# Dequantizing weight tiles in full width of 512 columns, beside attention over 6272 keys

## What is computed

```python
x = x + xattn(layernorm(x), ctx_4096, ...)   # 32 query heads, 8 key/value heads of 128, 6272 keys
x = x + attn(layernorm(x), ...)              # four 512x512 and three 512x1792 quantized matrices, with LoRA
x = x + ffn(layernorm(x), ...)

def _dequant(codes, scales):                 # codes 0..15, one scale per 64 weights
    w = NF4[codes]
    O, I = w.shape
    w = w.reshape(O, I // BLOCK, BLOCK) * scales[:, :, None]
    return w.reshape(O, I)
```

## Time and profile before

| | us |
|---|---|
| median of three runs (range) | 1162.08 (1157.77 to 1168.44) |
| the profiled execution, whole time | 1156.21 |
| its span, first to last instruction | 1154.4 |
| PE busy | 1079.8 (94%) |
| DVE busy | 945.8 (82%) |
| POOL busy | 627.0 (54%) |
| ACT busy | 444.6 (39%) |
| stretch 0 to 52 us (prologue) | 52 |
| stretch 1055 to 1154 us (most of `tail`) | 99 |

### The profile page before, as it was taken

The page is one execution under the profiler, slowest core; times in us unless marked ns, Lnnn a source line. Parts: engine busy times, 40 slices in busy tenths (PEclk is TensorE's granted clock), DMA queues, the critical chain, the costliest instruction groups (busy, mean ns, idle before and its releaser), DMA issues. The chain is left out here.

```text
span 1154.4 us, 23709 instructions
## 1 busy us (share of the span) xinstructions
PE 1079.8 (94%) x7035; PEld 954.4 (83%) x7035; DVE 945.8 (82%) x2331; ACT 444.6 (39%) x993; POOL 627.0 (54%) x1303
## 2 busy tenths in 40 slices
PE   6889999999999999899999999999999999995587
PEld 4889989899899989799899889998999999982132
DVE  3358998889988889888899888999898998884365
ACT  2134444344443444334443434444434443431030
POOL 2036675665666666656656666657666556652100
PEclk9689999999999999999999999999999999996879
DMA  9512121112212122121221221212221111114991
GB/s 358 201 38 70 57 63 59 60 53 71 59 47 72 55 61 62 53 59 51 65 63 51 64 65 50 70 41 62 72 63 49 56 43 51 47 46 161 337 379 55
DMA packets 66852, 99.26 MB, mean 86 GB/s; under 512 B 7780, under 2 KB 34916, under 8 KB 65956
## 3 DMA queue, kind: packets, MB, share of 16 engines
q1 hardware_dynamic: 63954, 86.97, 23.9%
q10 hardware_dynamic: 2178, 8.34, 2.1%
q0 software_dynamic: 592, 2.40, 0.6%
HBM read 82.79 MB, written 14.89 MB: 85 GB/s over the span
## 5 line engine op out<-in xcount | busy, mean ns | idle before, releaser
L439 POOL TENSOR_SCALAR leaf<-bit 128x256 f32<-128x256 uint16 x896 | 402.4, 449 | 113.0 <-DVE bit L776 29.1
L788 DVE COPY_PREDICATED leaf<-bit,leaf 128x256 f32<-128x256 uint16 x784 | 388.4, 541 | 50.4 <-POOL leaf L439 14.6
L461 POOL TENSOR_TENSOR leaf<-leaf,scale 128x256 f32<-128x256 f32 x112 | 81.2, 735 | 185.3 <-DVE leaf L788 184.4
L644 ACT ACTIVATE v_hi<-p_kv 128x256 fp32r<-128x256 f32 x196 | 75.2, 384 | 175.6 <-PE p_kv L61 175.5
L59 PE MATMUL p_kv<-wkv_hi,ctx_even_hi 128*128 128x256 f32 x448 | 128.1, 286 | 5.6 <-DVE v_lo L727 4.6
L644 ACT ACTIVATE k_hi<-p_kv,bk_sb 128x448 fp32r<-128x448 f32 x112 | 70.8, 632 | 156.6 <-PE p_kv L61 156.1
L739 DVE TENSOR_TENSOR pt_lo<-p_t,pt_hi 128x512 fp32r<-128x512 f32 x224 | 128.8, 611 | 1.6 <-ACT pt_hi L655 1.2
L655 ACT ACTIVATE pt_hi<-p_t 128x512 fp32r<-128x512 f32 x224 | 115.0, 542 | 33.9 <-PE p_t L544 33.8
L60 PE MATMUL p_kv<-wkv_lo,ctx_even_hi 128*128 128x256 f32 x448 | 125.9, 281 | 0.0
L61 PE MATMUL p_kv<-wkv_hi,ctx_even_lo 128*128 128x256 f32 x448 | 125.7, 281 | 0.0
L727 DVE TENSOR_TENSOR v_lo<-p_kv,v_hi 128x256 fp32r<-128x256 f32 x196 | 82.2, 419 | 46.0 <-ACT v_hi L644 45.6
(11 more groups left out here) (190 smaller groups left out, 2523.7 us busy)
## 6 DMA issues: line engine op xcount, KB each, us to landing
code<-in_codes SPq DMA_DIRECT2D x56, 256.0 KB, 2.6
scale<-in_scales SPq DMA_DIRECT2D x112, 128.0 KB, 3.0
expanded_weights<-leaf SPq DMA_DIRECT2D x112, 128.0 KB, 1.7
wring<-expanded_weights SPq DMA_DIRECT2D x28, 512.0 KB, 12.5
ctx_st<-in_ctx_t SPq DMA_DIRECT2D x96, 112.0 KB, 2.1
wq_sb<-in_wq SPq DMA_DIRECT2D x8, 1024.0 KB, 14.0
wring<-in_wo SPq DMA_DIRECT2D x16, 512.0 KB, 12.4
stage<-in_wkv ACTq DMA_DIRECT2D x4, 1024.0 KB, 8.6
```

Source lines behind the costliest of these rows:

```text
L439: m = nc.gpsimd.tensor_scalar(leaf[:, b, slot, :], bit0[:, b * HW:(b + 1) * HW], NF4[2 * j + 1] - NF4[2 * j], NF4[2 * j], ALU.mult, ALU.add)
L461: nc.gpsimd.tensor_tensor(leaf[:, b, 4, :], leaf[:, b, 0, :], scale[:, b * HW:(b + 1) * HW], ALU.mult).then_inc(scaled, 1)
L644: nc.scalar.activation(dst, src, ACT.Identity, bias=0.0 if bias is None else bias).then_inc(kv_rounded, 1)
L788: return nc.vector.copy_predicated(leaf[:, b, slot, :], bit[:, b * HW:(b + 1) * HW], leaf[:, b, other, :])
```

## The change

`leaf` becomes five slots of the full 512 columns. Every select, leaf and scaling works on 128x512: 7 selects instead of 14, one scaling instead of two, one tile write instead of two. Of the eight leaves POOL keeps six, and ACT computes leaves 4 and 5 (`high_leaf`), with biases in a small tile that shares a buffer with `drop`. Semaphores are split up accordingly: `low_ready`, `high_act`, `high_pool`, `low_chosen`. The order on DVE, ACT, POOL and SP is new. The PE stream is unchanged.

```diff
-        leaf = sb(st, "leaf", [P, 2, 5, HW], F32)
+        leaf = sb(st, "leaf", [P, 5, TW], F32)
...
+            def high_leaf(n, k):
+
+                if k == 0:
+                    act.wait_ge(low_chosen, n + 1)
+                m = nc.scalar.activation(leaf[:, 1 + k, :], bit0[:], ACT.Identity, bias=high_base[:, k:k + 1],
+                                         scale=NF4[9 + 2 * k] - NF4[8 + 2 * k])
+                if k == 1:
+                    m.then_inc(high_act, 1)
...
                         if t == 1:
                             round_ctx(s, h, half, 0, last)
+                        if t in (3, 4):
+                            high_leaf(i, t - 3)
                 else:
+                    for k in range(2):
+                        high_leaf(i, k)
                     round_ctx(s, h, half, 3, last)
...
             def high_leaves(n):
+                wait_apart(pool, low_chosen, n + 1, pool_passed)
+                leaf_of(6, 3)
+                if not (isinstance(n, int) and n == 0):
+                    wait_apart(pool, weight_out, 16 * n, pool_passed)
+                leaf_of(7, 4).then_inc(high_pool, 1)
...
+            def high_by_bit1(n, part):
+                if part == 0:
+                    wait_apart(dve, high_act, n + 1, dve_passed)
+                    take(bit1, 1, 2)
+                else:
+                    wait_apart(dve, high_pool, n + 1, dve_passed)
+                    take(bit1, 3, 4).then_inc(choice, 1)
...
                 else:
-                    take_other_bits(i)
-                    low_by_bit1(i, 0)
-                    low_by_bit2(i, 0)
-                    low_by_bit1(i, 1)
+                    low_by_bit2(i)
...
+                if h % 2 == 1:
+                    for part in range(2):
+                        high_by_bit1(i, part)
+                    high_by_bit2(i)
+                    all_by_bit3(i)
                 split_keys(k_use(s, h, 0), k_bank(h, 0), nh, 0)
+                if h % 2 == 1:
+                    take_bit0(i + 1)
+                split_probs(i, 0)
+                split_probs(i, 1)
                 if h % 2 == 0:
-                    split_probs(i, 0)
-                    split_probs(i, 1)
-                    high_by_bit2(i, 1)
-                    all_by_bit3(i, 1)
-                else:
-                    low_by_bit2(i, 1)
-                    split_probs(i, 0)
-                    split_probs(i, 1)
-                    high_by_bit1(i, 0)
+                    low_by_bit1(i + 1, 0)
                 split_keys(k_use(s, h, 1), k_bank(h, 1), nh, 1)
                 if h % 2 == 0:
-                    take_bit0(i + 1)
+                    low_by_bit1(i + 1, 1)
                 split_probs(i, 2)
+                if h % 2 == 1:
+                    take_other_bits(i + 1)
                 split_probs(i, 3)
```

More of the change, by code:

```diff
@@ L375, in tile_out @@
             def tile_out(n):
-                for b in range(2):
-                    sp.wait_ge(scaled, 2 * n + b + 1)
-                    sp.dma_start(weights[n, :, b * HW:(b + 1) * HW], leaf[:, b, 4, :]).then_inc(weight_out[b], 16)
+                sp.wait_ge(scaled, n + 1)
+                sp.dma_start(weights[n], leaf[:, 4, :]).then_inc(weight_out, 16)
             codes_of(0, True)
@@ L393, in load @@
                             load_ctx(s + 1, piece + q, start and q == 0)
+                    more = not (last and pair == NKV // 2 - 1)
                     load(0)
-                    if not start:
-                        tile_out(n - 1)
-                        scales_of(n)
+                    if more:
+                        codes_of(n + 2)
                     load(1)
-                    if not (last and pair == NKV // 2 - 1):
-                        codes_of(n + 2)
-                    load(2)
                     tile_out(n)
                     scales_of(n + 1)
+                    load(2)
+                    if more:
+                        codes_of(n + 3)
                     load(3)
+                    tile_out(n + 1)
+                    if more:
+                        scales_of(n + 2)
                     load(4)
-                    if not (last and pair == NKV // 2 - 1):
-                        codes_of(n + 3)
                     piece += PAIR_PIECES[pair]
@@ L414, in _ @@
             chunk(NCH - 1, True)
-            tile_out(NB - 1)
-            for b in range(2):
-                sp.wait_ge(weight_out[b], 16 * NB)
+            sp.wait_ge(weight_out, 16 * NB)
         @block.gpsimd
@@ L445, in low_leaves @@
                 if not (isinstance(n, int) and n == 0):
[L446 to L448 removed]
+                    wait_apart(pool, scaled, n, pool_passed)
+                for j in range(3):
+                    leaf_of(j, j)
+                leaf_of(3, 3).then_inc(low_ready, 1)
             def high_leaves(n):
[L451 to L455 removed]
+                wait_apart(pool, low_chosen, n + 1, pool_passed)
[3 more added lines that the diff above has]
+                leaf_of(7, 4).then_inc(high_pool, 1)
             def apply_scales(n):
                 wait_apart(pool, scale_in, 32 * (n + 1), pool_passed)
[L459 to L462 removed]
+                wait_apart(pool, chosen, n + 1, pool_passed)
+                nc.gpsimd.tensor_tensor(leaf[:, 4, :], leaf[:, 0, :], scale[:], ALU.mult).then_inc(scaled, 1)
             def add_rowsum(i, h):
@@ L471, in add_rowsum @@
                 nc.gpsimd.tensor_tensor(denom[:, h, :], denom[:, h, :], rowsum[:, h % 4, :], ALU.add)
+            for j in range(2):
+                m = nc.gpsimd.memset(high_base[:, j:j + 1], NF4[8 + 2 * j])
+            m.then_inc(bases, 1)
             narrow(0, True)
@@ L482, in split @@
                             split_ctx(s + 1, piece + q, 1 - par)
-                    if not (isinstance(n, int) and n == 0):
-                        apply_scales(n - 1)
                     low_leaves(n)
+                    narrow(n + 1)
                     split(0)
                     high_leaves(n)
-                    narrow(n + 1)
                     add_rowsum(n, 2 * pair)
+                    apply_scales(n)
+                    low_leaves(n + 1)
                     split(1)
-                    apply_scales(n)
+                    if not (last and pair == NKV // 2 - 1):
+                        narrow(n + 2)
                     split(2)
-                    low_leaves(n + 1)
-                    split(3)
                     high_leaves(n + 1)
                     add_rowsum(n + 1, 2 * pair + 1)
-                    if not (last and pair == NKV // 2 - 1):
-                        narrow(n + 2)
+                    split(3)
+                    apply_scales(n + 1)
                     split(4)
@@ L675, in block_work @@
                 act.wait_ge(max_ready, i + 1)
-                nc.scalar.activation(alpha[:, par, :], drop[:], ACT.Exp).then_inc(alpha_ready, 1)
+                nc.scalar.activation(alpha[:, par, :], drop, ACT.Exp).then_inc(alpha_ready, 1)
                 for r in range(RT):
@@ L802, in high_by_bit1, with take @@
[L802 to L813 removed]
+            def take(bit, slot, other):
+                return nc.vector.copy_predicated(leaf[:, slot, :], bit[:], leaf[:, other, :])
@@ L887, in _ @@
                 block_work(NCH - 1, h, 0, False, True)
-            for b in range(2):
-                high_by_bit1(NB - 1, b)
-                high_by_bit2(NB - 1, b)
-                all_by_bit3(NB - 1, b)
             add_output(NB - 1, NKV - 1)
```

114 lines of the change are left out of this document (47 added, 67 removed).

## The result

The changed kernel takes 1330.18 us (median of 4 runs, 1327.31 to 1332.12) against 1163.35 for the kernel before on the same chip: ratio 1.143, interval 1.137 to 1.149. The profiled execution spans 1325.5 us, 171 more than before. The direction was predicted; 1215 and the range up to 1250 were not met.

The account below looks back on a forecast made before the run. PE was taken as the bound, DVE close behind. To the profiled 1156 us, odd blocks' loss of 73 less even blocks' return of 25 added 48, and half clock 11: 1215 us, range 1178 to 1250.

Parts of the forecast that it names:

- the place and the kind of the loss: Odd block: DVE waits 2.45 us for ACT's leaves, pt_lo comes late, PE is 2.7 us later per block.
- the prices of undisturbed work: 512-column instructions: select 0.73 us, ACT leaf 0.65, POOL leaf 0.65, scaling 1.27 to 1.47.
- bit 0 0.55 (0.590): Odd block, DVE between k_lo and the first pt_lo: bit 0's mask takes 0.55 us, from a row of 0.590.
- four masks to 545.2: Even block on DVE, after the last v_lo: three selects to 543.8, then four masks done at 545.2 us.
- four selects at 0.73 with POOL idle: Odd block, DVE: four selects on high leaves at 0.73 us each, since POOL has finished its leaves before ACT.
- the clock in one pair of three: Half clock behind PE's new stall in one pair of three: 9 x 1.3 = 11 us.
- the upper bound I gave: Bound on the half-clock loss behind PE's odd-block stalls: 27 x 1.4 = 38 us.
- even blocks 0.9 shorter: Even blocks: PE's 22.4 us of waits for v_lo, and a little more, come back, 0.9 us per pair.
- So 0 here: Even block after the last v_lo: the second k_lo starts at 548.4 us as before, so no change.
- with 0.5 gain ... and 1.0 loss: Bounds on the even block's tail: 0.5 us gain if POOL is quicker, 1.0 loss if its leaves take 0.90.
- +2.7 - 0.9 + 0.4 = 2.2: Per pair in us: odd block's loss 2.7, even block's return 0.9, the remaining term for half clock.
- Rival 2: Disturbed prices hold, selects 1.08 and POOL leaves 0.90 us, in odd blocks and even tails: 1280 us, chance 0.05.

Follow-up runs that it names:

- e7: Changed kernel with the odd tile's last low select moved into the even block before and ACT's two leaves ahead of the exponentials; 1208.41 us.
- e3: Kernel before with full-width leaves, selects, scaling and tile write alone, all leaves on POOL, old order as far as possible; 1169.93 us.
- e6: Changed kernel with POOL's scaling split into two instructions of 256 columns; 1314.77 us.
- e4: Changed kernel with POOL scaling only 2 of 512 columns and leaves made a thousand times smaller; 1249.54 us.
- e5: Changed kernel with bit 0 masked ahead of the last select, and the even blocks' other masks behind the second pt_lo; 1286.00 us.
- e1: Changed kernel plus 24 matmuls with unread results where PE waits in odd blocks; 1291.98 us.
- e10: Kernel of e5 with 16 of e1's filler matmuls in the odd blocks; 1276.33 us.
- e8: Changed kernel's full width and ACT leaves kept, order of all engines rewritten, only low selects ahead of pt_lo in odd blocks; 1137.35 us, 0.981 of the kernel before.
- e9: Kernel of e8 with leaves 4 and 5 on POOL again, nothing else changed; 1165.94 us.
- e2: Changed kernel with ACT's two leaves moved to POOL, ahead of its two high ones; 1318.40 us.

## Why the prediction was wrong where it was

**Right: the place and the kind of the loss.** The leaves of ACT were to end 4.0 us after `drop`; DVE's select behind them starts at 4.1. The idle time was to be 2.4 us, 28 times, 65 us in total; it is 2.7, 28 times, 76.7. Transposes of chunk 2 wait for `pt_lo`, odd blocks lose, even ones don't wait for `v_lo` any more. e7 confirms the mechanism by taking it away, and e3 shows that the order and not the width made the loss. The order on SP and POOL alone was not put to a test.

**Right: the prices of undisturbed work.** A select of 512 columns was put at 0.73 and takes 0.73 to 0.75, ACT's leaf at 0.65 and takes 0.7, POOL's leaf at 0.65 and takes 0.62, the scaling at 1.27 to 1.47 and takes 1.30.

**Wrong: bit 0 at 0.55 and each other mask at 0.28 ("bit 0 0.55 (0.590)", "four masks to 545.2").** Bit 0 takes 1.10 in the odd block, one mask of the even block some 1.4. I had used the mean of the kernel before without asking what made it nearly twice the other masks' 320. Both masks stand in the new order close behind the last select (in the odd block with one `k_lo` between), which is what POOL's scaling waits for. The Trainium skill, SBUF — State Buffer, section "SBUF: two separate sides", names beside DVE's instructions with two SBUF inputs those that run in a 2-port mode. By that rule a mask, which has one input, waits for the end of a POOL instruction that began before it, if it runs in such a mode. I had applied the rule only to selects. Rows agree: 0.28 alone, 0.58 beside a half scaling (e6), 1.10 beside a full one.

**Wrong: four selects at 0.73 with POOL idle.** They took 3.61 instead of 0.73 + 0.62 + 2 x 0.85 = 3.05. POOL had finished its leaves, as I said, but ACT's rounding of the context follows its leaves, and POOL splits that piece at 927.89, beside the second select. The second select takes 1.22 there and the other three 0.73 to 0.76. I had moved a wait and not asked what the same wait releases on POOL; that the split holds the select is read from the timeline, no run takes it away. With the mask (0.55 over its price) this makes `pt_lo` 1.1 us later than predicted: transposes at 9.95 after `drop`, not 8.8, so 3.6 later than before and not 2.45.

**Wrong: the clock in one pair of three.** It fell in 26 of 27, because the pause was longer than the one I had priced. The price of one, 1.4 us, was right: 38 us, the upper bound I gave. This error hangs on the first two, since e6, with 0.5 us less pause, has 21 stretches and e4, with 0.8 less, has 7. But the length of a pause alone does not decide it: the 1.85 us of e5's even blocks are followed by half clock in 17 of 27, the 2.7 us of e4 in 7.

**Wrong: even blocks 0.9 shorter, with "So 0 here" for the tail.** The values' 22.4 us did come back. But the tail, put at 0 "with 0.5 gain ... and 1.0 loss", cost more. From the end of the last `v_lo` to the start of the second `k_lo` I had 541.47 to 548.4, 6.9 us; the changed kernel takes 8.1 (median), and e1, with the clock held up, as much. Of these 1.15 us, 0.25 are a later start of the scaling, 0.3 the scaling and the four low leaves (4.2 instead of 3.9), and 0.6 the select on them, which is held to 1.19, and what follows it. The chain was the right one; I had priced every link of it as if undisturbed. The even block is 1.5 longer than before, 2.4 longer than predicted, of which 0.9 is the half clock that reaches into it (25.1 to 24.2 in e1). The 1.5 that are left are 28 x 1.5 = 42 us, the largest single error; beside the tail's 1.15 they hold 0.15 that the values gave back less than the 0.9 (0.76 in e1) and 0.1 behind the second `k_lo`.

**The sum.** Predicted for a pair: +2.7 - 0.9 + 0.4 = 2.2. Measured: 4.5 + 1.5 = 6.0. Of the 3.8 between them e1 gives 1.4 - 0.4 = 1.0 to the clock, and 1.5 are the even block's. In the odd block the mask took 0.55 more than its price, the four selects 0.55, and they began 0.1 later: 1.0 + 1.5 + 0.55 + 0.55 + 0.1 = 3.7. The terms of the odd block and the parts of the even one are read from the timeline; e5, e6 and e10 take away or shorten the mask's, e4 the scaling's, and no run takes away the selects' alone.

Rival 2 (disturbed prices, 5 in 100) was the nearest in kind. It had the selects and POOL's leaves disturbed, and what was disturbed was the masks and one select of four in the odd block, and the select on the low leaves in the even one; POOL's leaves kept 0.62. I gave it too little: a row that shows two prices for one instruction was already in the earlier trace rows.

## What to carry to other kernels

When an order is rewritten, ask of each instruction not only what it waits for, but what the one ahead of it releases on the other engine, and whether the two can run side by side; the place right behind a releasing instruction is the worst for a short one that the released engine holds up and others wait behind. In e7 the mask was held too and cost nothing, since the `pt_lo` behind it was still in time for PE. Fewer and wider instructions win nothing where the engine was not the bound (e3: 141 us of busy time saved, none gained), while taking two leaves off the engine that holds DVE up won 29 us in one order (e8 against e9) and lost 12 in another (the changed kernel against e2). A pause of PE is priced with the half clock that may follow it (here 1.4 us on top of 3.5).

## What the runs showed of the hardware that was not expected

A 16-bit mask of 512 columns on DVE takes 0.28 us alone. When a scaling runs on POOL it lasts about until that ends: 0.58 beside one of 0.73, 1.10 beside one of 1.3. In e7 the two often begin within 0.05 us of each other, and then one of them gives way: either the mask takes 1.4 and the scaling 1.28, or the mask takes 0.3 and the scaling 1.46.

How often half clock followed a pause of PE was not a matter of its length alone. Counting the 27 pairs (idle time of PE, median): behind 3.5 us in odd blocks 26 times (changed kernel), behind 3.0 us 21 times (e6), behind 2.7 us 7 times (e4), but behind 1.85 us in even blocks 17 times (e5) and 14 times (e10). Behind the filled pauses (e1) it came once between the first and the last block. What decides between these cases no run here shows.
